# A hybrid block on one core: gate and up pieces of the shared experts in different scan steps, and seven buffers for a step's feed and states

## The chip, the core and the metric

The kernel runs on one core of one Trainium2 chip. The metric is the device time of one execution in microseconds. TensorE is called PE below, VectorE DVE, ScalarE ACT, GpSimd POOL, and SyncE, whose queue issues most DMAs, SP.

## The reference

Four sublayers follow one another on x of shape (8, 512, 512) in float32: 8 sequences of 512 tokens of 512 channels. Each reads a layer-normalised x, and its result is added to x.

```
x = x + scan(norm(x))        # selective state-space scan
x = x + moe(norm(x))         # 64 routed experts, top 6, and shared experts
x = x + attention(norm(x))
x = x + moe(norm(x))         # the same weights again

scan:  dt = softplus(W_dt (W_x x) + b);  for each of 16 states n and each channel d
       h[t] = exp(dt[t] * a[d,n]) * h[t-1] + dt[t] * B[t,n] * x[t,d]
       y[t,d] = sum_n C[t,n] * h[t,n,d] + D[d] * x[t,d]
shared experts:  (silu(x @ sw_gate) * (x @ sw_up)) @ sw_down     # 512 -> 704 -> 512
```

The change concerns the first stage, in which the scan runs on DVE while PE also makes the shared experts of the second sublayer for sequences whose scan is done.

## The kernel before, in words

**Stages.** `scan_plan`, `expert_plan`, `attention_plan` and `front_plan` each write one list of items such as `("scan", k)` or `("sg", 0, q, j)`. Every engine walks the whole list in this order and issues the items for which it has a function, so the list is the program order of all queues. An engine executes its own queue strictly in order; semaphores stop it where an operand isn't there or a buffer isn't free.

**The scan.** A scan step k handles one block of 128 channels (a column c of four), one pair of the 16 states, and all 512 tokens of one sequence b. There are 8 x 32 = 256 steps, `STEPS` = 32 per sequence. Two columns are worked on alternately, 16 steps for each pair, so a column pair ends at steps 15 and 31 of a sequence. A step is:

- POOL `feed(k)` (L1872): dt x times B for both states, written into `hb[k % HB]`. It waits until PE has summed step k - HB out of that buffer.
- ACT `decay(k)` (L1720): exp(dt a) into two of three PSUM banks used in turn. The next decays wait until DVE has used a bank.
- DVE `scan(k)`: two TENSOR_TENSOR_SCAN (L1349), then the second state times C (L1358). The first state is multiplied by C on POOL in `weigh_c(k)` (L1880), or in every eighth step on DVE (L1355).
- PE `y_sum(k)` (L1004): eight transposing accumulations of the weighed states. The first step of a column also adds D x (L996).

In the list, step k holds `feed(k+2)`, `scan(k)`, `weigh_c(k)`, then at two steps behind a column's end `x1` (DVE L1364, which waits for the last `y_sum` of the column and adds it to x), then what lies beside the step, and last `sum(k-1)`. Behind each step's scan come therefore, on every engine, the items beside it, and `sum(k-1)` is queued on PE behind the matmuls of step k.

**What lies beside.** `prepare_track(b)` has the norm, the turning, the projections and the softplus of sequence b, in the 32 steps of sequence b - 1. `quad_track(q)` has the routing and the shared experts of sequence (quad) q, at steps counted from the start of sequence q + 1; 32 and more fall into the sequence after. Within one step the items that take something out of a PSUM bank (`TAKERS`) come first, and among them the order of the tracks stays. Those that matter here are:

- `sg` (PE L1054), the gate piece j of six: 4 matmuls of 512 columns, eight records in the trace as they are float32. `su` (L1075) is the up piece. The last pair (j = 5) is issued as one block at `sg` (L1061, L1063).
- `silu` (ACT L1747): silu of the gate piece, out of its bank into the one buffer `ssg`; it waits until `hid` of the piece before has read that buffer. It needs another activation table than the exponentials: a table load stands ahead of it, and another ahead of the next exponential.
- `hid` (DVE L1377, L1381 for j = 5): `ssg` times the up piece out of its bank.
- `soft_exp`, `soft_ln` (ACT L1694, L1700), `dt_sum` (DVE L1339): the softplus of the next sequence.
- `turn`, `turned` (PE L961, ACT L1662): the normalised rows turned for the next quad, in four blocks, and `apply` (ACT L1636), which normalises them.
- `gate` (PE L1025), `sd` (PE L1089, L1095) and `so` (DVE L1392): router logits, the down projection and its use.

**Banks.** All these products share a ring of three PSUM banks in the order in which the list makes them (`Ring`, `wait_bank`): a product waits until the one three places earlier has been taken. Around the gates the order is sg0 su0 soft soft sg1 su1 soft soft sg2 su2 sg3 su3 sg4 su4 sg5 su5 turn0 turn1 turn2. So `sg1` waits for `hid0`, `sg2` for `hid1`, `turn0` for `hid4`, `turn1` for `silu5`, `turn2` for `hid5`.

The steps are constants: `silu` j lies `SILU_LAG` = 2 steps behind its gate piece and `hid` j `HID_LAG` = 2 behind its up piece; the next quad's `apply` is beside step 3 of a sequence (35 in this quad's count), its turns are beside steps 5, 5, 5 and 6, and each `turned` one step later. Before, `GATES` is (23, 26, 29, 30, 32, 35) and `UPS` (23, 26, 29, 30, 33, 35).

The work of the last quads that doesn't fit into the 256 steps is done by hand-written lists behind the scan. The expert stages and attention follow with memory and orders of their own.

Of the kernel before, what the change touches and what calls it, by code (L numbers as in the profile page):

```python
# [16 lines left out]
BATCH, SEQ, H = 8, 512, 512  # L17
# [16 lines left out]
NEG = -1e30  # L34
SCALE = float(1.0 / np.sqrt(np.float32(HEAD)))
BANK = 512
ARENA = 52928

# [3 lines left out]
GROUPS = NSTATE // NG  # L44
STEPS = GROUPS * HC
NSTEP = BATCH * STEPS
HB = 5
BOTH_EVERY, BOTH_AT = 8, 4
NBC = 3
AHEAD = 2  # L50
# [11 lines left out]
PICK_AT = (22, 23, 24, 27, 33, 35, 37, 41)  # L62
GATES, UPS = (23, 26, 29, 30, 32, 35), (23, 26, 29, 30, 33, 35)
DOWNS = (40, 41, 43, 51)
TURN_LAG, DT_LAG, SILU_LAG, HID_LAG, SO_LAG = 1, 2, 2, 2, 2
FIRST_DT, FIRST_SOFT = (0, 0), (("soft_exp", 3), ("soft_ln", 4), ("dt_sum", 5), ("dtx", 6))
X1_BEHIND = 2
# [95 lines left out]
class Arena:  # L163
# [3 lines left out]
    def cut(self, shape, dt=FP32):  # L167
        n = int(np.prod(shape))
        words = n if dt in (FP32, I32) else (n + 1) // 2
        words = (words + 7) // 8 * 8  # L170
        assert self.at + words <= ARENA, (self.at, words)
        view = self.base[:, self.at:self.at + words]
# [127 lines left out]
def quad_track(q):  # L300

    f = ("F", 0, q)
    for name, at in FRONT:
        yield at, ((name, f) if name in ("stats_a", "stats", "rstd", "apply") else (name, 0, q))
    for c in range(HC):
        yield TURN_F[c], ("turn", f, c)
        yield TURN_F[c] + TURN_LAG, ("turned", f, c)
    if q % 2:
        yield FOLD, ("fold", 0, q // 2)
        yield FOLD + 2, ("folded", 0, q // 2)  # L310
        for n in range(PICKS):
            yield PICK_AT[n], ("pick", 0, q // 2, n)
    for j in range(SC):
        yield GATES[j], ("sg", 0, q, j)
        yield UPS[j], ("su", 0, q, j)
        yield GATES[j] + SILU_LAG, ("silu", 0, q, j)
        yield UPS[j] + HID_LAG, ("hid", 0, q, j)
    for t in range(QT):
        yield DOWNS[t], ("fetch", 0, q, t)
        yield DOWNS[t], ("sd", 0, q, t)  # L320
        yield DOWNS[t] + SO_LAG, ("so", 0, q, t)


def first_steps():
# [275 lines left out]
class Program:  # L600


    def __init__(self, nc, ctx, dram):
        self.nc, self.ctx, self.d = nc, ctx, dram
        self.signals = []
        base = ctx.enter_context(nc.sbuf_tensor("arena", [P, ARENA], FP32))
        self.bank = [ctx.enter_context(nc.psum_tensor(f"bank{i}", [P, BANK], FP32)) for i in range(8)]
# [117 lines left out]
    def scan_memory(self, sb):  # L725
# [10 lines left out]
        self.bc = [sb.cut([2, NG, SEQ]) for _ in range(NBC)]  # L736
        self.hb = [sb.cut([NG, SEQ]) for _ in range(HB)]

# [203 lines left out]
def tensor_engine(p, eng):  # L942
# [44 lines left out]
    def y_sum(k):  # L987
        b, c, g = step_of(k)
        s, w, each = b % 2, p.hb[k % HB], b * HC + c
        y = bank[Y_BANKS[c % 2]]  # L990
# [1265 lines left out]
```

## Time and profile before

| | |
|---|---|
| median of 3 runs | 3016.0 us (3014.9 to 3018.98) |
| the profiled execution | 3015.6 us, of which 3013.8 us are the span from the first to the last instruction |
| granted TensorE clock, mean | 0.956 |
| busy over the span | PE 90%, DVE 59%, POOL 49%, PE weight loads 48%, ACT 43% |
| scan stage | from 0 to about 1060 us |

The spans of the sequences in the scan stage can be read from the DVE row L1364, which ends each column: from 415 us on they come every 129 to 130 us.

### The profile page before, as it was taken

The numbers are of one execution on the slowest core, as the hardware profiler recorded it, in microseconds if no ns is written. First come the engines' busy times: TensorE is split into PE (matmuls) and PEld (weight loads), VectorE is DVE, ScalarE is ACT, GpSimd is POOL, SyncE is SP. The second block draws the span as 40 slices with busy tenths as digits, with TensorE's granted clock in tenths as the row PEclk, the third lists the DMA queues.
The fourth block names the chain that finished last, engine by engine and source line by source line (L and its number), as shares of the span: only waits on it lengthen the run. The fifth ranks groups of instructions, "written<-read, shape, count | busy, mean of one in ns | idle before, by whom it ended". The sixth has DMA issues, their size and how long they took to land.

```text
span 3013.8 us, 37461 instructions
## 1 busy us (share of the span) xinstructions
PE 2720.2 (90%) x13484; PEld 1435.0 (48%) x13484; DVE 1772.6 (59%) x3835; ACT 1281.5 (43%) x2693; POOL 1483.1 (49%) x912
## 2 busy tenths in 40 slices
PE   4668888988889879999969999999899999999998
PEld 3454555545555534433335555555544444444443
DVE  5898999999899952222236666665624444222222
ACT  4657566665756411111127676666712220111111
POOL 5999989988998802222135555554500001121211
PEclk7779999999999889999989999999999999999999
DMA  5454555545554369999940000001135324899997
GB/s 187 153 184 154 185 167 166 187 142 195 166 176 164 131 265 358 396 393 393 392 121 1 29 29 29 29 29 42 64 100 189 118 79 159 308 381 338 359 337 218
DMA packets 168234, 566.13 MB, mean 188 GB/s; under 512 B 22832, under 2 KB 24752, under 8 KB 167536
## 3 DMA queue, kind: packets, MB, share of 16 engines
q1 hardware_dynamic: 149904, 521.65, 47.0%
q0 software_dynamic: 17088, 40.90, 5.9%
q8 instruction: 106, 1.74, 0.2%
q10 hardware_dynamic: 1056, 1.18, 0.1%
q14 instruction: 80, 0.66, 0.1%
HBM read 487.89 MB, written 75.79 MB: 187 GB/s over the span
## 4 chain that ended last, share of the span: by engine, by line
PE 53%; DVE 3%; ACT 2%; POOL 2%; DMA 2%; issue 1%; POOLq 0%; SPq 0%; DVEq 0%; ACTq 0%
PE bank L1151 10%; PE bank L1054 5%; PE bank L1075 5%; PE bank L1177 5%; PE bank L1089 5%; PE bank L1202 5%; PE bank L1259 4%; PE bank L1236 3%; PE bank L1224 2%; PE bank L1248 2%; POOL arena L1970 2%; DMA scratch_y<-arena 2%; PE bank L1134 1%; PE bank L1190 1%; ACT arena L1791 1%
## 5 line engine op out<-in xcount | busy, mean ns | idle before, releaser
L1872 POOL TENSOR_TENSOR arena<-arena 128x1024 f32<-128x1024 f32 x256 | 603.9, 2363 | 55.7 <-PE bank L1004 50.4
L1720 ACT ACTIVATE bank<-arena 128x512 f32<-128x512 f32 x512 | 344.5, 689 | 345.2 <-DVE arena L1349 184.7
L1970 POOL TENSOR_TENSOR arena<-arena 128x2048 f32<-128x2048 f32 (+3 forms) x128 | 296.9, 2323 | 275.0 <-DVE arena L1584 274.9
L1004 PE MATMUL bank<-arena 128*128 128x128 f32 x2048 | 296.7, 299 | 104.7 <-POOL arena L1880 103.5
L1791 ACT ACTIVATE arena<-arena 128x256 f32<-128x256 f32 (+3 forms) x512 | 287.1, 565 | 148.6 <-DVE arena L1575 124.9
L1349 DVE TENSOR_TENSOR_SCAN bank<-bank,arena 128x512 f32<-128x512 f32 x288 | 344.7, 1207 | 1.6 <-ACT bank L1720 1.1
L1004 PEld LDWEIGHTS bank<-arena 128*128 128x128 f32 x2048 | 258.0, 154 | 179.7 <-POOL arena L1880 128.5
L1151 PE MATMUL bank<-arena 128*64 128x352 f32 x2048 | 323.8, 470 | 0.0
L1054 PE MATMUL bank<-arena 128*128 128x512 f32 x640 | 298.2, 610 | 18.7 <-DVE arena L1377 18.7
L1075 PE MATMUL bank<-arena 128*128 128x512 f32 x640 | 288.7, 594 | 6.7 <-DVE arena L1339 6.7
L1880 POOL TENSOR_TENSOR arena<-arena 128x512 f32<-128x512 f32 x224 | 286.5, 1279 | 4.7 <-DVE arena L1349 4.5
L1349 DVE TENSOR_TENSOR_SCAN arena<-bank,arena 128x512 f32<-128x512 f32 x224 | 271.8, 1213 | 27.2 <-POOL arena L1872 14.5
L1089 PE MATMUL bank<-arena 128*128 128x512 f32 x640 | 286.5, 599 | 0.0
L1938 POOL DMA_INDIRECT arena<-scratch_xn,arena x64 | 68.7, 1073 | 440.8 <-DVE arena L1543 242.4
L1575 DVE CUSTOM_DVE_ANT_0 arena<-bank,arena 128x256 f32<-128x256 f32 (+3 forms) x512 | 220.9, 487 | 23.7 <-PE bank L1224 15.8
L1151 PEld LDWEIGHTS bank<-arena 128*64 128x64 f32 x2048 | 143.5, 139 | 147.6 <-issue 143.6
L1516 DVE TENSOR_TENSOR arena<-arena,bank 128x352 f32<-128x352 f32 x64 | 33.3, 521 | 306.9 <-issue 178.6
L1377 DVE TENSOR_TENSOR arena<-arena,bank 128x512 f32<-128x512 f32 x80 | 54.7, 683 | 244.5 <-PE bank L1075 243.7
L1075 PEld LDWEIGHTS bank<-arena 128*128 128x128 f32 x640 | 120.4, 190 | 160.2 <-issue 144.7
L1780 ACT ACTIVATE arena<-bank,arena 128x512 f32<-128x512 f32 x64 | 44.0, 687 | 346.7 <-PE bank L1177 324.2
L1054 PEld LDWEIGHTS bank<-arena 128*128 128x128 f32 x640 | 119.5, 195 | 149.9 <-issue 128.8
L1765 ACT ACTIVATE arena<-bank 128x352 f32<-128x352 f32 x64 | 29.7, 464 | 374.7 <-PE bank L1151 362.4
(145 smaller groups left out, 4187.9 us busy)
## 6 DMA issues: line engine op xcount, KB each, us to landing
arena<-scratch_bc SPq DMA_DIRECT2D x128, 1024.0 KB, 5.5
arena<-in_w_out SPq DMA_DIRECT2D x128, 768.0 KB, 15.3
arena<-in_w_gate SPq DMA_DIRECT2D x128, 704.0 KB
arena<-in_w_up SPq DMA_DIRECT2D x128, 704.0 KB
scratch_x<-arena SPq DMA_DIRECT2D x16, 1024.0 KB, 4.7
scratch_xn<-arena SPq DMA_DIRECT2D x15, 1024.0 KB, 4.6
arena<-scratch_x SPq DMA_DIRECT2D x44, 256.0 KB, 6.2
arena<-scratch_x SPq DMA_DIRECT2D x8, 1024.0 KB, 7.5
```

What stands on the lines that cost most here:

```text
L1004: i = nc.tensor.matmul(y[:, t * P:(t + 1) * P], w[:, n, t * P:(t + 1) * P], p.ident, is_transpose=True, start=False, stop=g == GROUPS - 1 ...
L1054: i = nc.tensor.matmul(out[:, :], f["swg"][:, c, j * P:(j + 1) * P], xnT[:, c, :], start=c == 0, stop=c == HC - 1)
L1075: i = nc.tensor.matmul(out[:, :], f["swu"][:, c, j * P:(j + 1) * P], xnT[:, c, :], start=c == 0, stop=c == HC - 1)
L1089: nc.tensor.matmul(out[:, :], f["shT"][:, j, t * P:(t + 1) * P], f["swd"][:, j, :], start=j == 0, stop=False)
L1151: i = nc.tensor.matmul(bank[1 + w][mine, 0:INTER], f["xeT"][k % 2][:, c, mine], f["ring"][(2 * k + half) % nw][w][:, c, :], start=c == 0, ...
L1349: nc.vector.tensor_tensor_scan(out=banks[n][:, :] if n or both else h[:, n, :], data0=banks[n][:, :], data1=h[:, n, :], initial=0.0, op0=A ...
L1575: nc.vector.tensor_tensor_reduce(out=p.sc[i % NSC][:, 0:width], in0=bank[c][:, 0:width], in1=p.amask[:, SEQ - width:], scale=-SCALE, scala ...
L1720: nc.scalar.activation(bank[p.da_bank(k, n)][:, :], block_of(p.dt, b, c), ACT.Exp, scale=p.alog[:, c, state:state + 1]).then_inc(*p.decaye ...
L1791: nc.scalar.activation(p.pr[n % 2][:, c, OFFSET[t]:OFFSET[t] + width], p.sc[i % NSC][:, 0:width], ACT.Exp, scale=-1.0, bias=p.nb[:, k % 2, ...
L1872: nc.gpsimd.tensor_tensor(out=p.hb[k % HB], in0=over(block_of(p.dtx, b, c), 1, NG), in1=p.bc[k // 2 % NBC][:, 0], op=ALU.mult).then_inc(*p ...
L1880: nc.gpsimd.tensor_tensor(out=h, in0=h, in1=p.bc[k // 2 % NBC][:, 1, 0, :], op=ALU.mult).then_inc(*p.weighted["pool"].up(k))
L1970: nc.gpsimd.tensor_tensor(out=own, in0=own, in1=over(p.rden[:, k % 2, :], 2, width), op=ALU.mult).then_inc(*p.divided.up(k))
```

## The change

In six of the seven quads handled in the scan stage (0 to 5) gate and up pieces are given steps of their own, (23, 26, 29, 31, 33, 36) and (24, 27, 30, 32, 34, 36); `silu` and `hid` follow by their lags. Quad 6 keeps the old steps. `HB` goes from 5 to 7, so that `feed(k)` waits for the sum of step k - 7. The two added buffers take 2048 words in each partition; they come from the scratch memory for the descriptors of software DMAs, which is set to 8192 bytes, and `ARENA` grows by as much. No instruction of an engine is added or taken away.

```diff
--- before.py
+++ after.py
@@ -34,7 +34,8 @@
 NEG = -1e30
 SCALE = float(1.0 / np.sqrt(np.float32(HEAD)))
 BANK = 512
-ARENA = 52928
+ARENA = 52928 + 2048
+DYNAMIC_SCRATCH = 8192
 
 
 
@@ -44,7 +45,7 @@
 GROUPS = NSTATE // NG
 STEPS = GROUPS * HC
 NSTEP = BATCH * STEPS
-HB = 5
+HB = 7
 BOTH_EVERY, BOTH_AT = 8, 4
 NBC = 3
 AHEAD = 2
@@ -62,6 +63,8 @@
 PICK_AT = (22, 23, 24, 27, 33, 35, 37, 41)
 GATES, UPS = (23, 26, 29, 30, 32, 35), (23, 26, 29, 30, 33, 35)
 DOWNS = (40, 41, 43, 51)
+APART = ((23, 26, 29, 31, 33, 36), (24, 27, 30, 32, 34, 36), DOWNS)
+SHARED_AT = [APART] * (BATCH - 2) + [(GATES, UPS, DOWNS)]
 TURN_LAG, DT_LAG, SILU_LAG, HID_LAG, SO_LAG = 1, 2, 2, 2, 2
 FIRST_DT, FIRST_SOFT = (0, 0), (("soft_exp", 3), ("soft_ln", 4), ("dt_sum", 5), ("dtx", 6))
 X1_BEHIND = 2
@@ -310,15 +313,16 @@
         yield FOLD + 2, ("folded", 0, q // 2)
         for n in range(PICKS):
             yield PICK_AT[n], ("pick", 0, q // 2, n)
+    gates, ups, downs = SHARED_AT[q]
     for j in range(SC):
-        yield GATES[j], ("sg", 0, q, j)
-        yield UPS[j], ("su", 0, q, j)
-        yield GATES[j] + SILU_LAG, ("silu", 0, q, j)
-        yield UPS[j] + HID_LAG, ("hid", 0, q, j)
+        yield gates[j], ("sg", 0, q, j)
+        yield ups[j], ("su", 0, q, j)
+        yield gates[j] + SILU_LAG, ("silu", 0, q, j)
+        yield ups[j] + HID_LAG, ("hid", 0, q, j)
     for t in range(QT):
-        yield DOWNS[t], ("fetch", 0, q, t)
-        yield DOWNS[t], ("sd", 0, q, t)
-        yield DOWNS[t] + SO_LAG, ("so", 0, q, t)
+        yield downs[t], ("fetch", 0, q, t)
+        yield downs[t], ("sd", 0, q, t)
+        yield downs[t] + SO_LAG, ("so", 0, q, t)
 
 
 def first_steps():
@@ -2248,7 +2252,7 @@
     from concourse.bass_utils import run_bass_kernel_spmd
 
     arrays = lay_out(inputs)
-    nc = bacc.Bacc("TRN2", target_bir_lowering=False, num_devices=1)
+    nc = bacc.Bacc("TRN2", target_bir_lowering=False, num_devices=1, dynamic_dma_scratch_size=DYNAMIC_SCRATCH)
     declare(nc, arrays)
     r = run_bass_kernel_spmd(nc, [{f"in_{n}": a for n, a in arrays.items()}], core_ids=[0])
```

## Rows read from the trace of the kernel before

Columns of a timeline row: start in us, duration in us, engine, line, operation, what it writes and reads, how many records; in brackets the idle time of its engine just before it and what ended that. Columns of a windows row: the stretch and its length, then busy us (and instructions) of PE, PE weight loads, DVE, ACT and POOL, the granted TensorE clock, the DMA share and GB/s.

**Rows 1.** windows, 543 to 672 us: busy us (instructions) per engine, granted clock, DMA share, GB/s

```profile
543.00:672.00 129.00, 115.31 (x525) 69.22 (x524) 123.28 (x165) 84.89 (x126) 117.29 (x70) 0.97 0.52 174
```

**Rows 2.** waits of DVE, 36 to 1055 us: total us, times, longest us

```profile
DVE arena L1364 <- PE bank L1004: 19.9, 8, 4.4
DVE arena L1349 <- POOL arena L1872: 14.5, 10, 4.9
DVE arena L1349 <- ACT bank L1720: 12.4, 13, 2.0
```

**Rows 3.** waits of POOL, 36 to 1055 us

```profile
POOL arena L1872 <- PE bank L1004: 50.4, 28, 4.2
```

**Rows 4.** timeline, 644 to 658 us (quad 3): start us, us, engine, line, tiles [idle before]

```profile
644.01 0.68 DVE L1377 TENSOR_TENSOR arena<-arena,bank 128x512 f32<-128x512 f32 x1
...
644.74 4.25 PE L1054 MATMUL bank<-arena 128*128 128x512 f32 x6 [2.72 <-DVE arena L1377]
...
647.44 0.69 DVE L1358 TENSOR_TENSOR arena<-bank,arena 128x512 f32<-128x512 f32 x1
...
651.20 1.28 ACT L1747 ACT_TABLE_LOAD   x1
...
657.63 1.22 DVE L1349 TENSOR_TENSOR_SCAN arena<-bank,arena 128x512 f32<-128x512 f32 x1
```

**Rows 5.** timeline, 518 to 529 us (quad 2)

```profile
518.09 0.69 DVE L1358 TENSOR_TENSOR arena<-bank,arena 128x512 f32<-128x512 f32 x1
...
521.85 1.28 ACT L1747 ACT_TABLE_LOAD   x1
...
528.29 1.22 DVE L1349 TENSOR_TENSOR_SCAN arena<-bank,arena 128x512 f32<-128x512 f32 x1 [1.31 <-ACT bank L1720]
```

**Rows 6.** timeline, 657 to 675 us (quad 3, end of a column pair)

```profile
657.77 3.70 PE L1054 MATMUL bank<-arena 128*128 128x512 f32 x8 [1.57 <-DVE arena L1377]
...
674.58 0.69 DVE L1364 TENSOR_TENSOR arena<-arena,bank 128x512 f32<-128x512 f32 x1 [3.01 <-PE bank L1004]
```

**Rows 7.** timeline, 555 to 560 us (quad 2) and 686 to 692 us (quad 3)

```profile
555.20 2.93 ACT L1636 ACTIVATE arena<-arena 128x512 f32<-128x512 f32 x4 [0.22 <-POOL arena L1857]
...
555.48 0.69 DVE L1358 TENSOR_TENSOR arena<-bank,arena 128x512 f32<-128x512 f32 x1
...
558.04 1.90 ACT L1720 ACTIVATE bank<-arena 128x512 f32<-128x512 f32 x3
...
559.66 1.23 DVE L1349 TENSOR_TENSOR_SCAN bank<-bank,arena 128x512 f32<-128x512 f32 x1
...
686.09 0.69 DVE L1358 TENSOR_TENSOR arena<-bank,arena 128x512 f32<-128x512 f32 x1
...
691.67 2.33 DVE L1349 TENSOR_TENSOR_SCAN bank<-bank,arena 128x512 f32<-128x512 f32 x2
```

**Rows 8.** timeline, 697 to 700 us (quad 3)

```profile
697.46 0.69 DVE L1358 TENSOR_TENSOR arena<-bank,arena 128x512 f32<-128x512 f32 x1
...
698.19 0.69 DVE L1381 TENSOR_TENSOR arena<-arena,bank 64x512 f32<-64x512 f32 x1
...
698.93 1.13 PE L961 MATMUL bank<-arena 128*128 128x128 f32 x4 [0.54 <-DVE arena L1381]
...
699.85 1.56 ACT L1662 COPY arena<-bank 128x512 f32<-128x512 f32 x3
```

**Rows 9.** windows, 644.7 to 650 us, where the gate piece of rows 4 runs

```profile
644.70:650.00 5.30, 5.26 (x9) 2.22 (x10) 4.91 (x6) 3.77 (x6) 5.30 (x3) 0.68 0.57 198
```

**Rows 10.** timeline, another gate piece, 384 us (quad 1)

```profile
384.08 3.70 PE L1054 MATMUL bank<-arena 128*128 128x512 f32 x8 [2.72 <-DVE arena L1377]
```

**Rows 11.** groups by line: count, busy us, mean ns, idle before it

```profile
L1747 ACT ACT_TABLE_LOAD x48 | 61.6, 1283 | 2.6 <-DVE arena L1377 1.9
...
L1747 ACT ACTIVATE arena<-bank 128x512 f32<-128x512 f32 x96 | 57.3, 596 | 244.9 <-PE bank L1054 194.3 <-PE bank L1063 30.0 <-DVE arena L1377 13.2
...
L1938 POOL DMA_INDIRECT arena<-scratch_xn,arena x64 | 68.7, 1073 | 440.8 <-DVE arena L1543 242.4 <-DVE arena L1507 124.0 <-DVE arena L1490 44.2
```

## The prediction

> **What bounds the kernel now.** I read the windows by stage first, then the waits of DVE, POOL and PE inside the scan stage, and then the timeline around the shared experts of one odd and one even quad. The change touches the scan stage alone (0 to about 1060 us of a span of 3013.8); behind it the same instructions run in the same order. In a settled sequence of this stage DVE is busy 123.3 of 129 us, POOL 117.3 and PE 115.3, ACT only 84.9 [rows 1]. DVE has the least room, and nearly every microsecond by which its idle time grows or shrinks is one of the span. Its whole idle time between 36 and 1055 us is some 49 us in three parts [rows 2]: 19.9 us before `x1`, for PE's last sum of a column; 14.5 us for POOL's feed, which the timeline has in sequence 0 and the beginning of 1 alone, where nothing of a quad runs yet; 12.4 us for ACT's decays, beside the softplus and `silu`. So a gain is capped: all of it would be 1.6% of the time, and what this change can reach, the first part, is 19.9 us.
>
> POOL does wait 50.4 us for PE's sums before its feeds [rows 3], which is what seven buffers take away. But each feed is made two steps ahead, and behind sequence 1 no scan of DVE waits for one. That time is slack of POOL, not of the span.
>
> **The seven buffers by themselves: 0.** They remove up to 50.4 us of POOL's idle time. What is late next is PE's sum itself, at the same place: the longest waits of POOL fall where DVE waits for the same sum in `x1` [rows 6]. The bounds are a gain of 50.4 and a cost of nothing, for POOL gets no new wait; I take 0, since DVE's row for POOL [rows 2] lies ahead of the quads. The smaller descriptor scratch touches the software DMAs. The gathers' POOL instructions have 440.8 us of idle time before them [rows 11], in the expert stages, so a wait for the ring up to that size is hidden; no row shows one. I take 0, with at most a few microseconds above.
>
> **Pieces in steps of their own.** No instruction is added; what moves is when banks come free, and three in-order queues hang on that. I go through a quad from its step 25 (w is the start of DVE's L1358 of a step, and quad 3 stands for the odd, quad 2 for the even ones).
>
> *Step 1, gate piece 1, +1.8.* `sg1` needs the bank that `hid0` frees. `hid0` moves from step 25 to 26, behind that step's scan. PE starts the piece 0.73 us behind the start of `hid` (644.01 to 644.74) [rows 4], so at w26 + 0.6 + 0.73 = w26 + 1.34, and has made it 3.6 later (the duration of such a piece at full clock, 3.70 with its first load) [rows 10]: w26 + 4.94. `silu1` started at w26 + 3.76 in both quads (651.20 - 647.44; 521.85 - 518.09) [rows 4, 5]; now it starts 1.2 us later. Behind it on ACT stand, in order, the softplus with its table loads and the next decays; DVE's scan comes 6.43 us behind that start (657.63 - 651.20; 528.29 - 521.85), and in the even quad it already waited 1.31 for it, in the odd one it had no room. So the scan of step 29 begins 1.2 later, and `hid1`, which stood ahead of it, is still owed, 0.6: 1.8 lost in each.
>
> *Step 2, gate piece 2, +0.5.* The same once more. `hid1` moves from step 28 to 29, so `sg2` is made at w29 + 4.94. `silu2`, a table load, a silu (1283 and 596 ns) [rows 11], the load back and a decay (1.90 us for three) [rows 7] take 3.9 us, to w29 + 8.9. DVE, with `hid1` and two `dt_sum` in step 29 and nothing in 30, would be there at w29 + 8.4.
>
> *Step 3, the wait in `x1`, -0.3.* This is what the change could win. From the start of `sg2` to `x1` are 16.8 us, of four pieces and three sums [rows 6]. Now three pieces stand ahead of the same sum: 13.3. But the start itself has moved from w28 to w29 + 1.34. `x1` begins at w29 + 14.7, and DVE wants it at w29 + 11.9. The wait is 2.7 where it was 3.0.
>
> *Step 4, `silu4` and `apply` together, +2.6 odd, +4.0 even.* `hid3` falls to step 34, `silu4` to 35, and `silu4` needs `hid3` out of the way (one buffer `ssg`). Before, `hid3` was at step 32 and `silu4` at 34, long ahead. Now ACT stands until w34 + 1.37 (0.6 to the start of `hid3`, 0.7 for it, 0.07). Behind the silu come in the same step `apply` of the next quad, 2.84 us (558.04 - 555.20) [rows 7], the table load and the decay of step 36: 1.28 + 0.6 + 2.84 + 1.28 + 0.64 + 0.1 = 6.75, so the scan of step 36 can't begin before w34 + 8.1. DVE needs it at w34 + 5.58 where picks stand between (691.67 - 686.09) and at w34 + 4.18 where they don't (559.66 - 555.48) [rows 7].
>
> *Step 5, the last pair and the turns, +3.7.* `hid5` moves from step 37 to 38, but `turn2`, which takes its bank, stays beside step 37, and `turned2` stays beside 38, on ACT ahead of the decays of step 39. So DVE's scan of 39 waits for a chain that begins in DVE's own step 38: `hid5` 0.73 behind w38, `turn2` 0.74 behind that, `turned2` 0.93 behind that (699.85 - 698.93, less a wait of none), all as in [rows 8]; then a copy of 0.6, the table load of 1.28 that until now stood ahead of the copies, a decay of 0.64, two handovers of 0.1: w38 + 5.1. Without the chain it is w38 + 1.4. Ahead of `turn2` PE also holds back the sums of 36 and 37; feeds with five buffers would come close to them, with seven they don't. So the buffers are the cover of this step; without it up to 2 us more.
>
> *The clock.* In quad 3 the gate piece after 2.72 us of waiting took 5.2 us (to 650), at a granted clock of 0.68, between the levels of 1.2 and 2.4 GHz [rows 4, 9]; that is 1.8 more than at 2.4; in quad 1 after the same wait it took 3.7 [rows 10]. The waits of `sg1` and `sg2` now become 4 to 7 us (in quad 3 PE stood from 644.74 - 2.72 = 642.0 on, and `sg1` would start at 648.8). Two pieces in each of six quads at 0 to 1.8 us are 0 to 21.6; I take half, 10.8, since rows of the shorter wait go both ways.
>
> **The sum.** Odd quads 1.8 + 0.5 - 0.3 + 2.6 + 3.7 = 8.3, even ones 9.7; three of each are 54.0, with the clock 64.8. The profiled execution took 3015.6 us, 0.4 under the median of the runs: 3015.6 + 64.8 = 3080. Quad 6 and the end of the stage, where PE is the bound, keep their steps; they only shift.
>
> **A rule of the Trainium skill.** Repeated gaps on POOL ahead of its feeds are the plainest pattern of the stage, 28 of them [rows 3]. "Perfetto Trace Analysis", section "Optimization Strategy", says that consistent bubbles on the engine that should be saturated can mean too few buffers. Taken for POOL, this speaks for the seven buffers, and it is rival (e). The trace has DVE as the saturated engine [rows 1], where the rule finds little.
>
> **The rivals.**
> (a) *Only some of the new waits reach DVE*: steps 1 and 2 are covered, because the silus find their pieces in time, and no clock is lost; steps 4 and 5 remain. 3 x (2.6 + 3.7) + 3 x (4.0 + 3.7) - 2 = 40 us: 3056. For it: step 2's margin is half a microsecond. Against it: step 1 has a row for each of its parts.
> (b) *Faster*: PE reaches the column's last sum before DVE does, as three pieces instead of four stand ahead of it, and DVE's wait in `x1` goes, 19.9 us at most: 2996. It decides if `sg2` starts at most 1.5 us behind w28, as it did. For it: it is the largest wait of DVE, and PE's two pieces in one step make it. Against it: `sg2` hangs on `hid1`, which has moved back a step, and the new waits of steps 4 and 5 come all the same.
> (c) *No change*: all of it is slack, as ACT has 44 us of it in each sequence [rows 1]. Against it: ACT's slack lies elsewhere than in these steps. 3016.
> (d) *Worse*: each stall also pushes PE behind into the down projections, and DVE waits there too, another 3 us for each quad and more: above 3098.
> (e) *Faster by the buffers*: POOL is what the stage goes by, DVE's idle time only a shadow of it, and the 50.4 us come off: 2965. Against it: DVE would have to lose more idle time than the 49 us it has [rows 2].
>
> **How the numbers follow.** My forecast, 3063 to 3098 for its own range (54 less a miss of 7, to 76 with a miss of 6), 0.58. (a), 3040 to 3063, 0.2. (b) 0.1, (c) 0.06, (d) 0.05, (e) 0.01. The range reaches to 3044 below and 3100 above; outside are (b), (c), (e), a little of (a) and half of (d), some 0.2. About 0.2%, 6 us, is what a measurement of this kernel can tell from none: faster 0.11, same 0.06, slower 0.83.
>
> **What would show it.** Step 1: at `silu1` ACT waits for L1054, and a scan behind it waits longer for L1720 than 1.31 us. Step 4: once per quad ACT waits for L1377 ahead of a table load followed by L1636, and DVE's scan waits 2.5 to 4 us. Step 5: once per quad ACT's third L1662 waits for L961, and DVE's scan then waits nearly 4 us. Step 3: L1364 still waits for L1004 in six places, 2.5 to 3 us each. The buffers: L1872's 50.4 us for L1004 nearly gone, outside quad 6. In all, DVE's waits for ACT grow from some 13 to some 70 us, and the sequences of quads 0 to 5 take about 140 us in place of 129.5. It is wrong if DVE's waits for ACT stay under 30 us, or if the wait in `x1` is gone.

## The result and the profile after

| | before | after |
|---|---|---|
| median | 3015.87 us (3014.9 to 3018.98, 4 runs) | 3092.37 us (3089.93 to 3095.11, 4 runs) |
| profiled execution, its span | 3015.6, 3013.8 us | 3095.11, 3093.3 us |
| granted clock, mean | 0.956 | 0.942 |

The changed kernel takes 1.0252 of the time [1.0237, 1.0268]: it is slower by 76.5 us. The forecast was 3080 (3044 to 3100). In its listing L1353 is the scan (L1349 before), L1359 and L1362 DVE's products, L1368 `x1`, L1876 the feed, L1884 `weigh_c`, L1724 the decay, L1008 the sum, L1058 and L1079 the gate and up pieces, L1381 and L1385 `hid`, L1751 `silu`, L1640 `apply`, L965 `turn`, L1666 `turned`.

The stage ends, with the last `x1`, at 1134.5 us where it ended at 1059.9: 74.6 of the 79.5 us between the two spans. Behind it the same work takes 1958.8 in place of 1953.9. The windows of one sequence, against [rows 1]:

```profile
575.00:718.00 143.00, 119.28 (x525) 70.72 (x524) 124.74 (x166) 85.41 (x125) 117.58 (x71) 0.93 0.48 156
```

A sequence takes 143 us where it took 129 to 130, DVE is 1.5 us busier and PE 4.0, and for each of the two the rest of the 13 us is idle time. The waits of DVE in the stage, 36 to 1135 us, against [rows 2]:

```profile
DVE arena L1353 <- ACT bank L1724: 50.9, 24, 3.9
DVE arena L1368 <- PE bank L1008: 28.8, 10, 5.9
DVE bank L1353 <- ACT bank L1724: 20.7, 7, 3.9
DVE arena L1353 <- POOL arena L1876: 20.3, 12, 4.9
```

The first and third row are the scans that wait for a decay: 71.6 us where 13.5 were (12.4 in [rows 2] and 1.1 on the form that writes a bank). `x1` had 28.6 us when the stretch is taken to the end of the stage, as it is here (36 to 1061). POOL's waits in the same stretch, against [rows 3]:

```profile
POOL arena L1884 <- DVE arena L1353: 103.4, 70, 4.2
...
POOL arena L1876 <- DMA arena<-scratch_bc: 8.5, 10, 2.9
```

The feed's 50.4 us for PE's sums are gone, as seven buffers should make them. POOL now waits twice as long for DVE's scan ahead of `weigh_c`. Quad 2 in DVE's timeline:

```profile
542.00 1.22 DVE L1353 TENSOR_TENSOR_SCAN arena<-bank,arena 128x512 f32<-128x512 f32 x1 [2.62 <-ACT bank L1724]
556.36 1.22 DVE L1353 TENSOR_TENSOR_SCAN arena<-bank,arena 128x512 f32<-128x512 f32 x1 [3.02 <-POOL arena L1876]
568.11 1.22 DVE L1353 TENSOR_TENSOR_SCAN arena<-bank,arena 128x512 f32<-128x512 f32 x1 [0.86 <-ACT bank L1724]
574.90 0.69 DVE L1368 TENSOR_TENSOR arena<-arena,bank 128x512 f32<-128x512 f32 x1 [3.65 <-PE bank L1008]
593.32 2.35 DVE L1353 TENSOR_TENSOR_SCAN bank<-bank,arena 128x512 f32<-128x512 f32 x2 [3.91 <-ACT bank L1724]
608.11 1.22 DVE L1353 TENSOR_TENSOR_SCAN arena<-bank,arena 128x512 f32<-128x512 f32 x1 [3.91 <-ACT bank L1724]
```

They are, in order, the scans of steps 26, 29 and 32, `x1`, and the scans of steps 36 and 39. Before, they waited 2.02, 1.31 [rows 5], nothing, 2.66, nothing and nothing; there was one more wait of 0.44, at the scan of step 38, which is gone. (At 556.36 feed and decay came together: the same wait is put down to ACT, 3.03, in the variant with five buffers below.) In the odd quad 3 they are 0.88, 2.61, 0.97, 3.65, 2.87 and 3.92. PE's gate pieces 1 and 2 of quad 2, against the 3.70 of [rows 6, 10]:

```profile
545.79 5.40 PE L1058 MATMUL bank<-arena 128*128 128x512 f32 x8 [4.52 <-DVE arena L1381]
...
560.08 5.29 PE L1058 MATMUL bank<-arena 128*128 128x512 f32 x8 [2.84 <-DVE arena L1381]
```

And ACT's side of steps 1, 4 and 5 in the same quad:

```profile
548.80 1.28 ACT L1751 ACT_TABLE_LOAD   x1
551.22 0.60 ACT L1751 ACTIVATE arena<-bank 128x512 f32<-128x512 f32 x1 [1.14 <-PE bank L1058]
...
586.51 1.28 ACT L1751 ACT_TABLE_LOAD   x1 [1.86 <-DVE arena L1381]
587.81 0.60 ACT L1751 ACTIVATE arena<-bank 128x512 f32<-128x512 f32 x1
588.30 2.92 ACT L1640 ACTIVATE arena<-arena 128x512 f32<-128x512 f32 x4
591.24 1.28 ACT L1724 ACT_TABLE_LOAD   x1
...
605.41 0.58 ACT L1666 COPY arena<-bank 128x512 f32<-128x512 f32 x1 [2.41 <-PE bank L965]
606.02 1.28 ACT L1724 ACT_TABLE_LOAD   x1
```

From 586.51 on stands step 4 as it was forecast: `silu4` behind `hid3`, `apply`, the load, the decay. From 605.41 on stands step 5: the third `turned` behind `hid5`, then the load. The first two rows are another matter. The table load of `silu1` didn't wait for the piece; only the silu did, 1.14 us, and the piece had taken 1.8 longer than the 3.60 of before, at a granted clock of 0.68 (545.79 to 551.19).

### The profile page after: what moved, and what is told of

It is laid out like the page before. It is cut to its first block, busy times and chain, and to the rows that moved or that the text cites. A ratio compares the mean times of both kernels' runs of the same rounds, so it can differ in the third digit from the quotient of the medians.

```text
span 3093.3 us, 37460 instructions
## 1 busy us (share of the span) xinstructions
PE 2742.1 (89%) x13484; PEld 1442.9 (47%) x13484; DVE 1784.3 (58%) x3835; ACT 1281.6 (41%) x2693; POOL 1482.6 (48%) x912
## 4 chain that ended last, share of the span: by engine, by line
PE 52%; DVE 3%; ACT 2%; POOL 2%; DMA 2%; issue 1%; POOLq 0%; SPq 0%; DVEq 0%; ACTq 0%
PE bank L1155 10%; PE bank L1181 5%; PE bank L1058 5%; PE bank L1079 5%; PE bank L1093 5%; PE bank L1206 5%; PE bank L1263 3%; PE bank L1240 3%; PE bank L1228 2%; PE bank L1252 2%; POOL arena L1974 2%; PE bank L1138 1%; PE bank L1194 1%; DMA scratch_y<-arena 1%; PE bank L1065 1%
## 5 line engine op out<-in xcount | busy, mean ns | idle before, releaser
L1876 POOL TENSOR_TENSOR arena<-arena 128x1024 f32<-128x1024 f32 x256 | 603.4, 2364 | 12.0 <-DMA arena<-scratch_bc 8.5
L1724 ACT ACTIVATE bank<-arena 128x512 f32<-128x512 f32 x512 | 343.6, 688 | 337.7 <-DVE arena L1353 187.9
L1008 PE MATMUL bank<-arena 128*128 128x128 f32 x2048 | 297.6, 298 | 90.3 <-POOL arena L1884 88.8
L1058 PE MATMUL bank<-arena 128*128 128x512 f32 x640 | 312.0, 633 | 52.1 <-DVE arena L1381 52.1
L1353 DVE TENSOR_TENSOR_SCAN bank<-bank,arena 128x512 f32<-128x512 f32 x288 | 344.7, 1207 | 21.2 <-ACT bank L1724 20.7
L1008 PEld LDWEIGHTS bank<-arena 128*128 128x128 f32 x2048 | 259.5, 154 | 173.4 <-POOL arena L1884 108.2
L1884 POOL TENSOR_TENSOR arena<-arena 128x512 f32<-128x512 f32 x224 | 285.3, 1274 | 104.0 <-DVE arena L1353 103.4
L1353 DVE TENSOR_TENSOR_SCAN arena<-bank,arena 128x512 f32<-128x512 f32 x224 | 271.8, 1214 | 71.3 <-ACT bank L1724 50.9
L1079 PE MATMUL bank<-arena 128*128 128x512 f32 x640 | 287.8, 592 | 0.0
L1093 PE MATMUL bank<-arena 128*128 128x512 f32 x640 | 286.3, 599 | 0.0
L1579 DVE CUSTOM_DVE_ANT_0 arena<-bank,arena 128x256 f32<-128x256 f32 (+3 forms) x512 | 220.9, 487 | 24.7 <-PE bank L1228 16.4
L1058 PEld LDWEIGHTS bank<-arena 128*128 128x128 f32 x640 | 124.7, 204 | 192.5 <-issue 137.5
L1381 DVE TENSOR_TENSOR arena<-arena,bank 128x512 f32<-128x512 f32 x80 | 54.7, 683 | 244.4 <-PE bank L1079 243.7
L1362 DVE TENSOR_TENSOR arena<-bank,arena 128x512 f32<-128x512 f32 x256 | 176.5, 690 | 14.4
```

Of the source, the lines that this page charges most:

```text
L1008: i = nc.tensor.matmul(y[:, t * P:(t + 1) * P], w[:, n, t * P:(t + 1) * P], p.ident, is_transpose=True, start=False, stop=g == GROUPS - 1 ...
L1058: i = nc.tensor.matmul(out[:, :], f["swg"][:, c, j * P:(j + 1) * P], xnT[:, c, :], start=c == 0, stop=c == HC - 1)
L1079: i = nc.tensor.matmul(out[:, :], f["swu"][:, c, j * P:(j + 1) * P], xnT[:, c, :], start=c == 0, stop=c == HC - 1)
L1093: nc.tensor.matmul(out[:, :], f["shT"][:, j, t * P:(t + 1) * P], f["swd"][:, j, :], start=j == 0, stop=False)
L1353: nc.vector.tensor_tensor_scan(out=banks[n][:, :] if n or both else h[:, n, :], data0=banks[n][:, :], data1=h[:, n, :], initial=0.0, op0=A ...
L1579: nc.vector.tensor_tensor_reduce(out=p.sc[i % NSC][:, 0:width], in0=bank[c][:, 0:width], in1=p.amask[:, SEQ - width:], scale=-SCALE, scala ...
```

## The experiments

The theory to test: the loss comes from where the silus and hids now stand, each of steps 1, 2, 4 and 5 by itself, with the clock on top; the buffers cost nothing. (A "rest" of PE is the idle time just before a piece.) The rivals: the pieces apart are a cost in themselves; the buffers or the smaller scratch cost; the waits are one chain, in which one taken away comes back at the next. Times stand beside the kernel before in the same series: its median there was 3014.4 (first four), 3017.0 (e5 to e8), 3015.1 (e9 to e11) and 3015.3 (e12). The cuts of code show the lines that carry the change; "..." stands for what is left out.

**e1, the seven buffers alone.**

```
-SHARED_AT = [APART] * (BATCH - 2) + [(GATES, UPS, DOWNS)]
+SHARED_AT = [(GATES, UPS, DOWNS)] * (BATCH - 1)
```

> Seven buffers and the smaller descriptor scratch, all pieces in their old steps. My theory: the buffers take POOL's 50 us of waiting for PE's sums away and give the span nothing, 3016 (within 3 us), since DVE waits for no feed behind sequence 1; DVE's wait in x1 stays at some 19 us. Rival A: POOL's waits were part of what bounds the stage, 2970 to 3000. Rival B: the 4.9 us by which the stages behind the scan were longer in the changed kernel's profile come from the smaller scratch, so 3021 here too.

Measured: 3026.16 us (3019.29 to 3030.34), 1.0046 [1.0029, 1.0063], against an expected 3016. So the buffers, or the scratch that pays for them, are not free. DVE's waits don't say why: they add up to less than before. Its busy time does, 958.7 us in the stage (36 to 1064) where 951.3 were. The groups that grew, first before and then e1 (window 36 to 1055; count, busy us, mean ns):

```profile
L1423 DVE TENSOR_TENSOR arena<-arena 128x256 f32<-128x256 f32 x7 | 6.0, 859 | 0.2
L1443 DVE TENSOR_SCALAR arena<-arena 128x256 f32<-128x256 f32 x7 | 5.8, 828 | 0.2
L1414 DVE TENSOR_SCALAR arena<-arena 128x4 f32<-128x4 f32 x7 | 5.2, 742 | 0.2
```

```profile
L1447 DVE TENSOR_SCALAR arena<-arena 128x256 f32<-128x256 f32 x7 | 11.3, 1613 | 0.2
L1418 DVE TENSOR_SCALAR arena<-arena 128x4 f32<-128x4 f32 x7 | 6.8, 965 | 0.2
L1427 DVE TENSOR_TENSOR arena<-arena 128x256 f32<-128x256 f32 x7 | 6.6, 939 | 0.2
```

One of the masks (L1443, L1447), in the timeline of before and of e1:

```profile
738.37 1.28 POOL L1880 TENSOR_TENSOR arena<-arena 128x512 f32<-128x512 f32 x1
739.12 0.68 DVE L1443 TENSOR_SCALAR arena<-arena 128x256 f32<-128x256 f32 x1
739.60 2.40 POOL L1872 TENSOR_TENSOR arena<-arena 128x1024 f32<-128x1024 f32 x1
```

```profile
737.58 2.35 POOL L1876 TENSOR_TENSOR arena<-arena 128x1024 f32<-128x1024 f32 x1
737.63 2.46 DVE L1447 TENSOR_SCALAR arena<-arena 128x256 f32<-128x256 f32 x1
```

And another of e1's masks, which begins just ahead of a feed:

```profile
605.25 0.29 DVE L1447 TENSOR_SCALAR arena<-arena 128x256 f32<-128x256 f32 x1
605.26 2.48 POOL L1876 TENSOR_TENSOR arena<-arena 128x1024 f32<-128x1024 f32 x1 [0.22 <-DMA arena<-scratch_bc]
```

The same instruction takes 0.29 us when it begins ahead of POOL's, 0.68 when it begins in the second half of `weigh_c`, and 2.46 when it begins just behind the start of a feed: it ends 0.15 us behind POOL's instruction (739.93 and 740.09). Before, six of the seven masks of the stage began in the second half of a `weigh_c`; in e1 five of the seven begin inside a feed. What the buffers took away, in the time before these instructions, are POOL's waits for PE, and with them the order in which POOL's and DVE's instructions met. So the price is one of timing, of who is beside whom; it doesn't follow from the number of buffers alone. The Trainium skill says in "SBUF — State Buffer", section "SBUF: two separate sides", of the port pair that VectorE and GpSimd share that it "is an exclusive lock, not a bandwidth split"; by that rule a DVE instruction that needs the pair would last as long as the feed ahead of it, and the trace agrees, with 2.46 beside 2.35. DVE's 512 scans, which read a PSUM bank too, took only 0.2 us more in all. It is so in the traces of all fourteen kernels: of 247 instructions of these three groups that began inside one of POOL's, 246 ended 0.02 to 0.36 us behind it.

**e2, the pieces apart on five buffers and the full scratch.**

```
-ARENA = 52928 + 2048          +ARENA = 52928
-HB = 7                        +HB = 5
...
```

> Pieces apart with five buffers, memory and scratch as in the kernel before. My theory: the pieces are the whole of the 76 us, and the buffers only cover that PE holds sums back behind sg1, sg2 and turn2; without that cover POOL's feeds wait for PE and the time is 3092 to 3105, mostly near 3095. Rival: the seven buffers themselves do harm, then this is clearly below 3092, down to 3080.

Measured: 3086.24 us (3084.99 to 3087.75), 1.0241 [1.0223, 1.0258], under the 3092 to 3105 that were expected. Going back to five buffers cost nothing. The median is 6 us under that of the changed kernel, which is what the rival said, but the intervals of the two ratios overlap. DVE's busy time in the stage is clearer: 954.4 us up to the end of the last `x1`, 8.2 under that of the changed kernel. POOL waits longer than ever for PE, and it costs nothing (waits of POOL, 36 to 1128):

```profile
POOL arena L1876 <- PE bank L1008: 83.7, 55, 4.6
```

DVE's waits in quad 2 are 2.62, 3.03, 0.83, 3.65, 3.91 and 3.91, as with seven. So the buffers were no cover for step 5 either.

**e3, hid0 and hid1 back** in steps 25 and 28, everything else as changed (in e3, e5, e7, e8, e9, e11 and e12 the lines stand two further down than in the changed kernel: L1355 scan, L1370 `x1`, L1060 and L1081 pieces, L1383 `hid`).

```
+SILUS_APART, HIDS_APART = (25, 28, 31, 33, 35, 38), (25, 28, 32, 34, 36, 38)
...
```

> The changed kernel with hid of pieces 0 and 1 back at steps 25 and 28, so one step behind their up pieces. My theory: sg1 and sg2 get their banks a step earlier; DVE's waits for ACT at steps 29 and 32 shrink by 2.5 and 1.0 us (even quads) or go (odd), and as only three pieces now stand between that sg2 and the column's last sum, the wait of 3.64 us in x1 goes as well: some 7.4 us for each of six quads, 44 in all, 3048. Rival: the pieces in steps of their own are late by themselves, and the bank only appears as the releaser; then hardly anything moves, 3080 to 3092.

Measured: 3051.48 us (3045.86 to 3056.51), 1.0131 [1.0114, 1.0148]: 41 us come back. DVE's waits (36 to 1120):

```profile
DVE arena L1355 <- ACT bank L1726: 34.2, 17, 3.9
DVE bank L1355 <- ACT bank L1726: 20.7, 7, 3.9
DVE arena L1355 <- POOL arena L1878: 14.4, 10, 4.9
DVE arena L1370 <- PE bank L1010: 8.1, 7, 6.0
```

The decays cost 16.7 us less than in the changed kernel, `x1` 20.7 less and POOL's rows 5.9 less. This is what the change could win: with `sg2` at its old time, three pieces ahead of the sum leave 0.34 of the wait in `x1` in even quads and 0.03 in odd ones (of the 8.1, 6.0 are at the end of the stage).

**e11 and e12, hid0 back alone and hid1 back alone.**

```
e11: +SILUS_APART, HIDS_APART = (25, 28, 31, 33, 35, 38), (25, 29, 32, 34, 36, 38)
e12: +SILUS_APART, HIDS_APART = (25, 28, 31, 33, 35, 38), (26, 28, 32, 34, 36, 38)
...
```

> The changed kernel with hid0 alone back in its step (25 in place of 26); hid1 stays in 29, and everything else too. Both back took 3051, 41 less than the changed kernel. Theory (step 1 by itself, gate piece 1 late for its silu): 6 x 1.8 = 11 less, 3081, the scan of step 29 waits 1.3 in even quads in place of 2.6; x1's six waits of 3.6 stay, since gate piece 2 hangs on hid1 alone; what is left, 30 us, is hid1's. Rival (the two are one delay: PE is late for gate piece 2 because it was late for 1): most of the 41 us, 3055 to 3065, and x1's waits go.

> The changed kernel with hid1 alone back in its step (28 in place of 29); hid0 stays in 26. hid0 back alone took 3090, both 3051. There the scan of step 29 waited less, but PE then rested 6.9 us before gate piece 2 (before: 2.8), the piece took 6.6 us in place of 5.3, and the scan of step 32 waited 2.1 to 2.3 us in place of 0.9. Theory (hid1 holds most of the cost, and hid0's delay is hidden only while hid1 is late as well): with hid1 back, step 1's price of 1.8 a quad shows in full, so 3051 + 6 x 1.8 = 3062; x1's six waits of 3.6 are gone, and the scan of 29 waits 2.6 in even quads. Rival (hid0's delay costs nothing wherever it stands): 3051 to 3054. Second rival (the two interact so that either alone keeps the loss): above 3075.

Measured: e11 3090.15 us (3084.32 to 3093.03), 1.0243 [1.0228, 1.0258]; e12 3065.33 us (3064.7 to 3068.91), 1.0164 [1.0151, 1.0178]. With hid0 late as well as hid1 3092, with hid1 late alone 3090, with hid0 late alone 3065, with neither 3051. hid0 costs 14 us where hid1 is in time and 2 where it isn't; the 11 us that e11 was to bring back didn't come. Its quad 2 on PE and DVE, at steps 29 to 32:

```profile
557.51 6.55 PE L1060 MATMUL bank<-arena 128*128 128x512 f32 x8 [6.71 <-DVE arena L1383]
```

```profile
566.80 1.22 DVE L1355 TENSOR_TENSOR_SCAN arena<-bank,arena 128x512 f32<-128x512 f32 x1 [2.12 <-ACT bank L1726]
573.59 0.69 DVE L1370 TENSOR_TENSOR arena<-arena,bank 128x512 f32<-128x512 f32 x1 [3.64 <-PE bank L1010]
```

Piece 1 is in time, so PE rests 6.71 us ahead of piece 2 where it rested 2.84, and piece 2 takes 6.55 where it took 5.29. The scan of step 32 waits 2.12 where it waited 0.86: the 1.26 of the piece, to the hundredth. Over the six quads the waits of step 29 fall from 16.4 to 7.3 us and those of step 32 rise from 5.4 to 11.4. `x1` waits 3.64 as before, whether piece 2 takes 5.33 or 6.75: what the clock adds to piece 2 is in the wait of step 32.

In e12's quad 2 piece 1 ran at full clock (granted 1.00) behind a late hid0:

```profile
536.10 3.70 PE L1060 MATMUL bank<-arena 128*128 128x512 f32 x8 [3.35 <-DVE arena L1383]
...
539.12 1.28 ACT L1753 ACT_TABLE_LOAD   x1
540.41 0.60 ACT L1753 ACTIVATE arena<-bank 128x512 f32<-128x512 f32 x1
```

The silu stands right behind its table load, with no wait. At full clock step 1 doesn't hold up `silu1` at all. The expectation had the scan of step 29 wait 2.6 in even quads of e12; it waits at most 0.65 in any. The wait stands one instruction ahead, at hid1, which needs up piece 1, and that is made behind gate piece 1. In quad 0, where the gate piece took 6.13:

```profile
267.09 0.69 DVE L1383 TENSOR_TENSOR arena<-arena,bank 128x512 f32<-128x512 f32 x1 [3.00 <-PE bank L1081]
```

These waits are 11.0 us in all, 0.57 behind the piece of 3.70 and 2.26 behind one of 5.40: the clock again. They are most of the 14 us; 0.6 at each scan of step 26 comes on top, and the 1.3 that even quads of e3 wait at step 29 is gone.

**e4, the last pair back** in step 35, as one block.

```
-APART = ((23, 26, 29, 31, 33, 36), (24, 27, 30, 32, 34, 36), DOWNS)
+APART = ((23, 26, 29, 31, 33, 35), (24, 27, 30, 32, 34, 35), DOWNS)
```

> The changed kernel with the last pair of pieces back at step 35 (silu and hid at 37). My theory: the chain hid5, turn2, turned2, table load, decay, scan through step 38 is gone, 3.9 us in each of six quads, less 0.4 that even quads had before at step 38: 3070. Rival: ACT's table loads come two for each silu wherever it stands, so the wait moves to the neighbouring step and less than 8 us come back, 3084 or more.

**e5, silu4 back** in step 34, where it was before, with hid3 in 33 (before: 32).

```
+SILUS_APART, HIDS_APART = (25, 28, 31, 33, 34, 38), (26, 29, 32, 33, 36, 38)
...
```

> The changed kernel with the silu of piece 4 and the hids of pieces 3 and 4 one step earlier, as they stood against the scan before the change (silu4 in step 34, hid3 in 33, hid4 in 36); the pieces stay in steps of their own and the seven buffers stay. Theory (step 4 of the prediction: silu4 behind hid3, in one step with apply, holds up the decay of step 36): the one wait of 2.5 to 2.9 us (odd quads) or 3.9 us (even quads) of the scan for the decay goes, 3 x 2.7 + 3 x 3.9 = 20 us, so 3072 in place of 3092, and the other waits stay (3.9 us at step 39, 2.6 us at step 29 in even quads, 3.6 us in x1). Rival (the waits of a quad are one chain, PE behind by as much as it is: what is taken away at step 36 comes back at step 39): the wait at 39 grows by as much as the one at 36 shrinks, 3088 to 3092.

Measured: e4 3075.05 us (3070.14 to 3078.02), 1.0198 [1.0181, 1.0215]; e5 3077.06 us (3074.84 to 3077.72), 1.0201 [1.0187, 1.0216]. Each takes its own wait away and leaves the other's. In e4 the scan of step 39 in quad 2 has no wait (that of step 38 has 0.36, as the 0.44 of before) and that of step 36 still 3.91; in e5 it is the reverse, 3.91 at step 39 and no wait at 36. So they are two stalls, not one chain. But both times are some 5 us above what was expected. In e4 the waits of step 29 are 3.8 us more than in the changed kernel over the six quads. Gate piece 1 and DVE's waits at steps 26 and 29 of quad 2 in e5 show how:

```profile
540.13 6.75 PE L1060 MATMUL bank<-arena 128*128 128x512 f32 x8 [3.31 <-DVE arena L1383]
```

```profile
536.35 1.22 DVE L1355 TENSOR_TENSOR_SCAN arena<-bank,arena 128x512 f32<-128x512 f32 x1 [3.43 <-ACT bank L1726]
552.06 1.22 DVE L1355 TENSOR_TENSOR_SCAN arena<-bank,arena 128x512 f32<-128x512 f32 x1 [4.37 <-ACT bank L1726]
```

The piece takes 6.75 where it took 5.40, though PE rested less ahead of it, and the scan of step 29 waits 4.37 where it waited 3.02: 1.35 and 1.35. e4 has 6.73 and 4.35. The granted clock in the piece was 0.54 in e5, against 0.68. Nothing in the schedule of these steps differs from the changed kernel. e5's quad 4 has the other end, a piece 1 at full clock with hid0 and hid1 both late:

```profile
820.74 3.70 PE L1060 MATMUL bank<-arena 128*128 128x512 f32 x8 [3.31 <-DVE arena L1383]
...
830.19 1.22 DVE L1355 TENSOR_TENSOR_SCAN arena<-bank,arena 128x512 f32<-128x512 f32 x1 [1.89 <-ACT bank L1726]
```

Without any loss of clock the scan of step 29 still waits 1.89, 0.6 more than before; e11's even quads have 1.90 too, and its odd ones 0.52 where nothing stood. That is hid1, which no longer stands ahead of this scan.

**e6, the smaller scratch and larger arena alone; e10, the same with six buffers** (lines one further down than in the kernel before).

```
-ARENA = 52928                 +ARENA = 52928 + 2048
                               +DYNAMIC_SCRATCH = 8192
...
 e10 also: -HB = 5             +HB = 6
```

> The kernel before with the smaller descriptor scratch and the arena larger by 2048 alone; five buffers and the old steps. The kernel with all three (seven buffers too) took 1.0046 of the time before, 12 to 14 us, of which its DVE instructions beside POOL's feeds show some 8. Theory (the buffers do it: POOL's feeds, no longer held back by PE, run beside DVE's instructions): this one takes the time before, 3015, within 2 us. Rival (the smaller scratch makes the software DMAs wait for the ring, in the expert stages): 3019 to 3028, with the loss behind the scan stage.

> The kernel before with six buffers in place of five (and the smaller scratch, which by itself cost 1.0008 [0.9999, 1.0016]); old steps. Theory (what the buffers cost is how often POOL's feed runs just when DVE's instructions on SBUF do, so it follows POOL's waits for PE): POOL's wait between five's 50 and seven's none, and a time between 3017 and 3026, about 3021. Rival 1 (it is the place of the buffers in SBUF or the length of the rotation, not POOL's waiting): 3017 or 3026, whatever POOL's wait. Rival 2 (more buffers don't cost: the seven-buffer result was spread between runs): 3017.

Measured: e6 3019.37 us (3012.16 to 3023.77, 11 runs), 1.0008 [0.9999, 1.0016]; e10 3025.17 us (3021.36 to 3032.52), 1.0034 [1.0021, 1.0046]. The scratch by itself doesn't cost beyond the noise (2.4 us by the medians); the buffers do. The sixth already does it. In e10 (36 to 1055; POOL's wait, then DVE's groups):

```profile
POOL arena L1873 <- PE bank L1005: 3.4, 4, 1.4
```

```profile
L1444 DVE TENSOR_SCALAR arena<-arena 128x256 f32<-128x256 f32 x7 | 12.2, 1742 | 0.2
L1424 DVE TENSOR_TENSOR arena<-arena 128x256 f32<-128x256 f32 x7 | 11.0, 1572 | 0.2
```

POOL's wait for PE is gone with six as with seven, so this was no middle dose: it doesn't tell the theory from its first rival. The waits and the longer instructions go together in both. Of the 12 and 10 us that e1 and e10 cost by their medians, these groups carry some 8 in e1's profile and 13 in e10's.

**e7, the pieces ahead of `x1`'s sum alone**, on five buffers: up piece 3 two steps later and both pieces 4 one step later; every silu in its old step, and only hid3 a step later.

```
+APART = ((23, 26, 29, 30, 33, 35), (23, 26, 29, 32, 34, 35), DOWNS)
+SILUS_APART, HIDS_APART = (25, 28, 31, 32, 34, 37), (25, 28, 31, 33, 35, 37)
...
```

> The kernel before (five buffers, full scratch) with only three moves in quads 0 to 5: up piece 3 from step 30 to 32, gate piece 4 from 32 to 33, up piece 4 from 33 to 34; all silus and hids stay in the steps in which they were, but silu3 stays in 32 and hid3 goes from 32 to 33. Theory (the wait of 3.0 us in x1 is for the fourth piece of 3.6 us that PE makes ahead of the column's last sum, and what the change lost it lost by moving takers, not by moving pieces): three pieces stand ahead, the six waits in x1 of 3.0 us go and nothing else waits: 3015 - 18 = 2997. Rival 1 (PE is behind anyway, the sum comes no earlier or the piece moved behind it is late for its silu): 3012 to 3016. Rival 2 (clock: PE's longer rests lower it): 3016 to 3025.

**e8, all pieces but the last pair apart, with the takers back; e9, the same on five buffers.**

```
+APART = ((23, 26, 29, 31, 33, 35), (24, 27, 30, 32, 34, 35), DOWNS)
+SILUS_APART, HIDS_APART = (25, 28, 31, 33, 34, 37), (25, 28, 32, 33, 36, 37)
...
```

> The changed kernel with its pieces in steps of their own and seven buffers, but every silu and hid as near as can be to its step of before (hids 0 and 1 in 25 and 28, hid2 32, hid3 33, silu4 34, hid4 36, and the last pair in 35, silu and hid in 37). Theory (all of the loss is by the takers' steps, plus the cost of the buffers): the loss of steps 1, 2, 4 and 5 goes and the six waits in x1 go too, since three pieces stand ahead of the sum and the gate piece 2 starts at its old time: the seven-buffer kernel's 3026 less 18 = 3008. Rival (gate and up pieces apart are themselves a cost: each waits for DVE alone and PE's clock falls): 3026 to 3045.

> The pieces in steps of their own with the silus and hids near their old steps, as in the kernel that took 3010 with seven buffers, but with five buffers and the full descriptor scratch. Theory (seven buffers cost DVE some 8 us of longer instructions wherever they stand, and give nothing): 3000 to 3004, DVE busy 5 to 7 us less, POOL waiting for PE again, 30 to 80 us. Rival (the fourth piece moved out of x1's way is what lets POOL's feeds be of use, the buffers cover a wait of PE here): 3010 or more, with new waits of DVE for POOL's feed or for PE.

Measured: e7 3004.40 us (3000.84 to 3010.41), 0.9966 [0.9953, 0.9979]; e8 3009.94 us (3003.92 to 3016.8, 12 runs), 0.9978 [0.9968, 0.9988]; e9 3003.26 us (3000.39 to 3004.93), 0.9956 [0.9943, 0.9969]. All three beat both kernels. e7 missed its 2997 by 7 us. DVE's wait in `x1`, in the stage with its end (36 to 1120 in e7 and e8, 36 to 1060 in e9), in this order:

```profile
DVE arena L1370 <- PE bank L1010: 7.2, 4, 6.2
```

```profile
DVE arena L1370 <- PE bank L1010: 10.1, 5, 6.0
```

```profile
DVE arena L1370 <- PE bank L1010: 15.0, 8, 7.4
```

These stand against 28.6. In e7 21 us of waiting went, and its profiled execution is 14.8 us under that of before. The stage is 18.0 us shorter (its last `x1` at 1041.8), as forecast; new waits of 0.43 at step 33 in five quads and 3.2 us of longer DVE instructions took some of it back, and the work behind the stage took 3.3 more. What `x1` still waits in e8 and e9, beside the end of the stage, is 3.11 us behind a gate piece 2 of 6.77 in e8, and 2.99 and 3.00 behind two of 6.66 in e9. Pieces apart are no cost in themselves. e9 is 6.7 us under e8 by the medians, in two series, and their ratios just touch. DVE is busy 1776.5 us there against 1781.4, which is the buffers' price once more, though the two profiled executions themselves took as good as the same (3004.9 and 3004.2).

## Why the prediction came out as it did

The direction and the places of steps 4 and 5 were right; 3092 lies 12 us above the 3080. Steps 1 to 3 and the clock gave nearly the right sum for reasons that were partly wrong. DVE's new waits in the six quads, in us (difference to before; beside them the last wait of the stage fell by 2.6, and one of 0.9 came at a step 23):

| place | forecast | measured |
|---|---|---|
| step 1: scans of steps 26 and 29 | 10.8 | 3.6 + 12.5 |
| step 2: scan of step 32 | 3.0 | 5.4 |
| step 3: `x1` | -1.8 | 2.7 |
| the clock | 10.8 | within the rows above |
| step 4: scan of step 36 | 19.8 | 19.6 |
| step 5: scan of step 39, less the 0.44 at 38 | 22.2 | 22.2 |
| sum | 64.8 | 66.0 |

- *What bounds*: right. DVE's waits in the stage grew by 64 us (58.1 for decays, 5.8 on the rows of POOL, two of which are the decays of step 29, 0.2 in `x1` with the end of the stage) and its busy time by 11.7; the stage grew by 74.6.
- *Step 1, gate piece 1, +1.8 a quad*: 0.6 of it was right and 1.2 was not. The 0.6 for hid1, no longer ahead of the scan of step 29, is there: 1.89 with a full-clock piece in e5's quad 4 and 1.90 in e11, where before stood 1.31. The 1.2 was put on the piece's later start. But the table load runs ahead of the wait for the piece and covers that start: e12's quad 2 has no wait of `silu1` at full clock. What DVE lost beyond the 0.6 is the clock. In quads 0, 2 and 4 the piece takes 6.15, 5.40 and 5.40 and the scan waits 3.78, 3.02 and 3.02; in e5's quad 2 6.75 and 4.37. Of the 12.5, some 9 are clock (16.4 less the 7.3 of e11).
- *A term left out in step 1*: hid0, too, went behind a scan that was waiting for ACT. That of step 26 waits 0.6 more in each quad (2.62 for 2.02, 0.88 for 0.30), 3.6 in all. The 0.6 was counted for hid1 and not for hid0.
- *Step 2, +0.5*: a wait came, 0.80 to 0.97 in each quad where none stood, but not for the reason given. It is the length of gate piece 2 less 4.43 us in every quad here and in e11 (5.22 and 0.80, 5.40 and 0.97, 6.55 and 2.12). By that a piece of 3.7 would leave none; it is clock, and that the 0.5 came near is luck.
- *Step 3, the wait in `x1`, -0.3*: wrong in sign. It is 3.64 or 3.65 where it was 2.66 to 3.01 (and 4.42 in quad 1 before, behind a piece of 5.26, so the six together grew by 2.7 us only). The start of `sg2` was as forecast; the piece was counted at 3.6 and took 5.2 to 5.4 in all six quads. An estimate from the 4.43 above: at 3.7 some 0.7 less would be left in `x1`, 2.9, near the 2.7 of the forecast. No run had gate piece 2 at full clock with hid1 late.
- *Step 4, +2.6 odd and +4.0 even*: 2.52, 2.87 and 2.52 odd, 3.91 even. Right, and shown by e5.
- *Step 5, +3.7*: 3.91 to 3.92, where before nothing stood. Right, and shown by e4. Its "up to 2 us more" without the buffers was wrong: e2.
- *The clock, +10.8*: too low. The twelve pieces took 23.6 us above 3.6 each (13.2 in `sg1`, 10.4 in `sg2`) where the same twelve of before had 7.7. (The 5.2 that the prediction read for quad 3's piece is 5.40 in the trace.) Some 9 us of it reached DVE at step 29, 5.4 at step 32, and by the estimate above some 4 in `x1`. The sum held because two misses had opposite signs: a later start and an ACT chain that cost nothing, and a clock and a hid0 that cost more.
- *The seven buffers, 0*: wrong. By themselves seven cost 1.0046 and six 1.0034, 12 and 10 us; in the changed kernel they cost 6 us by e2's median and 8.2 of DVE's busy time. That is the larger part of the distance to 3092. The argument looked at who waits for whom. The cost is in no wait: it is in the durations of DVE's instructions.
- *The rivals*: (b) had a true core. Its condition, `sg2` at most 1.5 us behind w28, is met in e3, e7, e8 and e9 (1.33 in each), and there the wait in `x1` goes, but for three quads with a slow piece. (e) is turned round: POOL's 50.4 us went and the time rose.

What stays open: why the clock fell in one piece and not in another; whether the longer DVE instructions are all of the buffers' price; and the 4.9 us behind the stage, which are within what runs of this kernel differ by.

## What to carry to other kernels

When a producer is moved later in a schedule of fixed steps, list its taker, what that taker frees, and what stands in order behind the taker on its queue: here all pieces but the last pair could be spread at a gain (0.9956) so long as their takers kept their steps, and cost 2.5% when the takers moved with them. Of a bubble ahead of an engine, ask first whether its busy time is harmless where it would go: an engine that is no longer held back may come to stand beside instructions of the one that bounds, and lengthen them. After taking one stall away, look again at the durations next to it, not at the waits alone, before the gain is counted.

## What the hardware showed

- DVE's masks and products of 128x256 that read and write SBUF alone, and began while a POOL instruction ran, ended 0.15 to 0.36 us behind it, in all fourteen traces with one exception: 2.46 us beside a feed of 2.35, for one that takes 0.29 when it begins just ahead of a feed. DVE's scans, which read a PSUM bank too, showed nothing of it (0.2 us over 512).
- The granted clock of a piece isn't told by the length of the rest ahead of it. Behind 2.72 us a piece took 3.70 and 5.40 before; in the later runs it was 3.70 behind 3.35, 3.70 and 6.75 behind 3.31 in one and the same run (e5), 5.40 behind 4.52 and 6.55 behind 6.71. The granted clock was 1.00 in the pieces of 3.70, 0.68 in one of 5.40 and 0.54 in one of 6.75. A change elsewhere in the schedule went with 1.35 us more for a piece of quad 2; that it was the cause is not shown.
- A table load stood ahead of the wait for the piece that the silu reads: load at 548.80, silu at 551.22. So it hid up to 1.28 us of a late input. It did not stand ahead of the other wait, for hid3 to free `ssg`: there the load itself waited 1.86 (586.51).
